# Eight attention heads scored and mixed in a row, one PSUM ring of seven banks, and weight transfers moved at a change of layers

## The reference, cut to what matters

```
for i in range(6):
    x = attn_layer(shift_tokens(x), Wqkv[i], q_scale[i], k_scale[i], Wo[i]) + x
    x = ffn_layer(shift_tokens(x), ln_g[i], ln_b[i], W1[i], b1[i], W2[i], b2[i]) + x

attn_layer: q, k, v of 16 heads of 64; q and k are normalised, scaled and rotated
            sim = 8 * q k^T over windows of 64 queries and 128 keys, masked; softmax; out = attn v; out @ Wo
ffn_layer:  layer norm; h = xn @ W1 + b1; a * gelu(gate) @ W2 + b2   (inner size 682)
```

## Time and profile before

| what | value |
|---|---|
| median of 3 runs | 2676.1 us (2675.84 to 2676.21) |
| the profiled execution, its own time | 2678.44 us |
| its span | 2676.6 us |
| PE busy | 2590.3 us, 97% |
| DVE, ACT, POOL busy | 85%, 77%, 52% |
| mean granted TensorE clock | 0.989 |
| DMA, mean | 95 GB/s |

### The profile page before, as it was taken

One profiled execution on the slowest core, in us unless ns is written; L12 is line 12 of the kernel. 1 busy time (PEld: TensorE's weight loads), 2 busy tenths in 40 slices (PEclk: granted clock), 3 DMA queues, 4 the chain that ended last, 5 costly groups with the idle time before them and its releaser, 6 DMA issues.

```text
span 2676.6 us, 77877 instructions
## 1 busy us (share of the span) xinstructions
PE 2590.3 (97%) x25160; PEld 2304.0 (86%) x25160; DVE 2279.7 (85%) x7689; ACT 2060.1 (77%) x6056; POOL 1386.8 (52%) x1438
## 2 busy tenths in 40 slices
PE   8889999999999999999999999999999999999996
PEld 7768888888888888888888888888888888888886
DVE  5579989988998888899888989988898998888883
ACT  5468878877887777788877878877888888787774
POOL 5454545545464555455464645545454645555560
PEclk9999999999999999999999999999999999999998
DMA  5212232433223333322234232244222242311110
GB/s 172 75 52 92 71 117 91 140 97 126 92 70 110 116 106 122 117 90 72 98 129 157 71 116 86 77 150 143 89 73 97 92 158 68 97 32 31 42 27 26
DMA packets 149541, 253.24 MB, mean 95 GB/s; under 512 B 21418, under 2 KB 88202, under 8 KB 148106
## 3 DMA queue, kind: packets, MB, share of 16 engines
q1 hardware_dynamic: 148698, 250.90, 28.8%
q10 hardware_dynamic: 688, 0.39, 0.1%
HBM read 137.14 MB, written 80.55 MB: 81 GB/s over the span
## 4 chain that ended last, share of the span: by engine, by line
PE 87%; DVE 2%; issue 2%; DMA 1%; POOL 1%; SPq 1%; ACT 1%; DVEq 0%; ACTq 0%; POOLq 0%
PE ring L1123 29%; PE ring L1173 14%; PE acc L1148 10%; PE score L1214 7%; PE acc L1186 6%; PE ring L1227 6%; PE ring L1137 6%; PE mix L1241 4%; PE mix L1245 2%; PE mix L1243 2%; PE ring L1157 1%; DMA xn<-res 1%; PE ring L1105 1%; PE acc L1193 0%; DVE probs L1599 0%
## 5 line engine op out<-in xcount | busy, mean ns | idle before, releaser
L1123 PE MATMUL ring<-w_qkv,xT 128*128 128x512 f32 x3456 | 888.3, 402 | 5.8 <-DVE with_sin L1506 4.5
L1123 PEld LDWEIGHTS ring<-w_qkv,xT 128*128 128x128 f32 x3456 | 627.7, 190 | 133.5 <-DVE with_sin L1506 6.1
L1408 POOL TENSOR_SCALAR sums_sq<-sums_sq 128x8 f32<-128x8 f32 x384 | 109.1, 284 | 1078.6 <-DVE sums_sq L1501 1070.3
L1344 ACT ACTIVATE probs<-probs,shift 128x128 f32<-128x128 f32 x1536 | 596.6, 392 | 25.9 <-DVE shift L1583 25.2
L1583 DVE CUSTOM_DVE_ANT_0 probs<-score,mask,query_scale 128x128 f32<-128x128 f32 x1536 | 438.5, 346 | 42.2 <-PE score L1214 34.9
L1173 PEld LDWEIGHTS ring<-nT,w_up 128*128 128x128 f32 x3168 | 395.8, 189 | 21.4 <-issue 6.8
L1173 PE MATMUL ring<-nT,w_up 128*128 128x256 f32 x3168 | 409.6, 282 | 4.2 <-issue 3.6
L1289 ACT ACTIVATE with_sin<-ring 128x512 f32<-128x512 f32 x384 | 228.2, 595 | 212.8 <-PE ring L1123 212.8
L1417 POOL TENSOR_TENSOR sums_sq<-sums_sq,half 128x8 f32<-128x8 f32 x192 | 323.2, 1683 | 16.0
L1414 POOL TENSOR_TENSOR query_scale<-sums_sq,half 128x8 f32<-128x8 f32 x192 | 318.1, 1657 | 22.0 <-POOL sums_sq L1408 11.8
L1362 ACT COPY probsT<-ring 128x512 f32<-128x512 f32 x384 | 226.4, 594 | 100.9 <-issue 95.6
(11 more groups left out here) (153 smaller groups left out, 4424.4 us busy)
## 6 DMA issues: line engine op xcount, KB each, us to landing
w_parts_scratch<-staging SPq DMA_DIRECT2D x120, 519.0 KB, 3.1
staging<-in_w_next SPq DMA_DIRECT2D x60, 519.0 KB, 5.0
w_qkv<-w_parts_scratch SPq DMA_DIRECT2D x20, 1536.0 KB, 9.1
v_mid<-v SPq DMA_DIRECT2D x192, 128.0 KB, 2.3
w_up<-w_parts_scratch SPq DMA_DIRECT2D x20, 640.0 KB, 6.1
y_in<-y_scratch SPq DMA_DIRECT2D x48, 256.0 KB, 3.0
res<-y_scratch SPq DMA_DIRECT2D x48, 256.0 KB, 2.7
y_scratch<-res SPq DMA_DIRECT2D x41, 256.0 KB, 3.2
```

What stands on the lines that cost most here:

```text
L1123: last = pe.matmul(bank(item)[:], xT[a][:, h, t * P:(t + 1) * P], w_qkv[w][:, h, c, g, :], start=(h == 0 and (a, w) == PASSES[0]), stop=(h ...
L1344: last = act.activation(probs[:, k, cols], probs[:, k, cols], ACT.Exp, bias=shift[:, k, i:i + 1], scale=-1.0, accum_out=sums[:, k, i:i + 1])
```

## The change

Three things are done.

1. **Order.** The four quads are taken in twos: `scores 0` and `scores 1` stand next to each other, then `mix 2` and `mix 3` of the sequence before; later `scores 2`, `scores 3`, `mix 0`, `mix 1`. Both `mix 2` and `mix 3` are now done a slot later. `shift`, `sums`, `probs` and `probsT` hold eight heads in place of four. The lists of ACT and DVE are rewritten to suit; POOL's stays. (`gelu_table` in ACT's list emits nothing.)
2. **Banks.** Scores (two fills each) and mixes (one each) go through the ring, which has seven banks, with 49 fills a slot. `bank_free` has the two new kinds.
3. **Transfers.** The slot after a change of layers (8L+1, `new=True`) is written out for SP alone. The fetches of blocks 3, 4 and 5 move from slot 8L+8 to it: 3 and 4 behind the load of `res`, 5 behind the three shifting copies. The first two chunk loads of the next layer move from slot 8L+1 to slot 8L+8, behind the fetch of block 2. The program also gets a smaller scratch for dynamic DMAs, which none of these transfers uses.

```diff
-RING = 4
+RING = 7
 PE_ORDER = [
-    ("scores", 0), ("mix", 3), ("unit", 1, 0), ("unit", 1, 1), ("project_out", 0), ("unit", 1, 2), ("unit", 1, 3),
-    ("project_out", 1), ("turn", 1, 0), ("turned", 0, 0), ("turned", 0, 1),
-    ("scores", 1), ("mix", 0), ("turn", 1, 1), ("unit", 1, 4), ("unit", 1, 5), ("turn", 1, 3), ("turned", 1, 0), ("turn", 1, 2),
-    ("input",), ("turned", 1, 1), ("norm_turn",),
-    ("scores", 2), ("mix", 1), ("unit", 0, 0), ("gate", 0), ("gate", 1), ("unit", 0, 1), ("gate", 2), ("value", 0),
+    ("scores", 0),
+    ("scores", 1), ("mix", 2), ("mix", 3), ("unit", 1, 0), ("unit", 1, 1), ("unit", 1, 2), ("unit", 1, 3), ("project_out", 0),
+    ("project_out", 1), ("unit", 1, 4), ("unit", 1, 5), ("input",), ("turn", 1, 2), ("turn", 1, 0), ("turn", 1, 1),
+    ("turned", 0, 0), ("turned", 0, 1), ("turned", 1, 0), ("unit", 0, 0), ("turned", 1, 1), ("turn", 1, 3), ("norm_turn",),
+    ("scores", 2),
+    ("scores", 3), ("mix", 0), ("mix", 1), ("unit", 0, 1), ("gate", 0), ("gate", 1), ("unit", 0, 2), ("gate", 2), ("value", 0),
...
 ACT_ORDER = [
-    ("out", 3), ("unit", 1, 0), ("exp", 0, 0), ("unit", 1, 1), ("exp", 0, 1), ("unit", 1, 2), ("unit", 1, 3), ("scale", 0, 1),
-    ("split_high", 0, 0), ("copied", 0, 0), ("split_high", 0, 1), ("copied", 0, 1), ("turn", 1, 0), ("exp", 1, 0),
-    ("exp", 1, 1), ("turn", 1, 1), ("unit", 1, 4), ("unit", 1, 5), ("turn", 1, 3), ("copied", 1, 0), ("turn", 1, 2), ("out", 0),
+    ("out", 2), ("exp", 0, 0), ("out", 3), ("unit", 1, 0), ("exp", 0, 1), ("unit", 1, 1), ("split_high", 0, 0), ("unit", 1, 2),
+    ("exp", 1, 0), ("exp", 1, 1), ("unit", 1, 3), ("unit", 1, 4), ("unit", 1, 5), ("input",), ("scale", 0, 1), ("copied", 0, 0),
+    ("turn", 1, 2), ("copied", 0, 1), ("turn", 1, 0), ("turn", 1, 1), ("unit", 0, 0), ("copied", 1, 0), ("copied", 1, 1),
+    ("turn", 1, 3), ("norm_turn",), ("exp", 2, 0), ("out", 0), ("exp", 2, 1), ("out", 1), ("exp", 3, 0), ("unit", 0, 1),
...
 DVE_ORDER = [
-    ("mask", 0, 0), ("mask", 0, 1), ("out", 3), ("rotate", 1, 0), ("rotate", 1, 1), ("scale", 0, 0), ("inverse", 0, 1),
-    ("rotate", 1, 2), ("add_out",), ("rotate", 1, 3), ("mask", 1, 0), ("mask", 1, 1), ("norm_stats",), ("scale", 1, 0),
+    ("mask", 0, 0), ("mask", 0, 1), ("mask", 1, 0), ("out", 2), ("mask", 1, 1), ("out", 3), ("rotate", 1, 0), ("rotate", 1, 1),
+    ("scale", 0, 0), ("inverse", 0, 1), ("rotate", 1, 2), ("add_out",), ("rotate", 1, 3), ("scale", 1, 0), ("input",),
+    ("norm_stats",), ("scale", 1, 1), ("split_low", 0, 0), ("norm_apply",), ("rotate", 0, 0), ("mask", 2, 0), ("norm_turn",),
...
+assert len(RING_FILLS) % RING == 0
+RING_BANK = [_at % RING for _at in range(len(RING_FILLS))]
...
-def run_slots(eng, slot):
+def run_slots(eng, slot, apart=False):
...
-        with eng.Fori(1 if layer else 2, BATCH - 1) as b:
+        if layer and apart:
+            slot(Slot(layer * BATCH + 1, layer, next_batch=2, ffn_batch=0, chunk=0 if layer < DEPTH - 1 else None, new=True))
+        with eng.Fori(1 if layer and not apart else 2, BATCH - 1) as b:
...
-                if s.chunk is not None:
+                if s.new:
+                    fetch(3, s.layer - 1)
+                    fetch(4, s.layer - 1)
+                if s.chunk is not None and not s.new:
                     for h in range(SLOT_CHUNKS):
                         W.load_chunk(sp, s.layer, s.chunk, h)
...
+                if s.new:
+                    fetch(5, s.layer - 1)
                 if s.late:
                     load_mid(n, 1)
...
                 if s.switch == "ffn":
                     fetch(2, s.layer)
+                    if s.layer + 1 < DEPTH - 1:
+                        for h in range(SLOT_CHUNKS):
+                            W.load_chunk(sp, s.layer + 1, 0, h)
...
-                if s.switch == "ffn":
-                    fetch(3, s.layer)
-                    fetch(4, s.layer)
...
                 if s.switch == "ffn":
-                    fetch(5, s.layer)
                     load_params(s.layer + 1)
...
-                wait(pe, scores_masked, H)
-                pe.sem_inc(passed, 1)
+                for half in range(2):
+                    bank_free(s, item, half)
+                    pe.sem_inc(passed, 1)
...
-                pe.wait_ge(probs_scaled[j], s.n * 4 + k + 1)
+                pe.wait_ge(probs_scaled[2 * (k % 2) + j], s.n * 2 + k // 2 + 1)
```

More of the change, by code:

```diff
@@ L79 @@
+    ("turned", 3, 1),
 ]
 ACT_ORDER = [
-    ("out", 3), ("unit", 1, 0), ("exp", 0, 0), ("unit", 1, 1), ("exp", 0, 1), ("unit", 1, 2), ("unit", 1, 3), ("scale", 0, 1),
-    ("split_high", 0, 0), ("copied", 0, 0), ("split_high", 0, 1), ("copied", 0, 1), ("turn", 1, 0), ("exp", 1, 0),
-    ("exp", 1, 1), ("turn", 1, 1), ("unit", 1, 4), ("unit", 1, 5), ("turn", 1, 3), ("copied", 1, 0), ("turn", 1, 2), ("out", 0),
-    ("input",), ("copied", 1, 1), ("norm_turn",), ("exp", 2, 0), ("unit", 0, 0), ("exp", 2, 1), ("gate", 0), ("unit", 0, 1),
@@ new lines @@
+    ("turn", 1, 2), ("copied", 0, 1), ("turn", 1, 0), ("turn", 1, 1), ("unit", 0, 0), ("copied", 1, 0), ("copied", 1, 1),
+    ("turn", 1, 3), ("norm_turn",), ("exp", 2, 0), ("out", 0), ("exp", 2, 1), ("out", 1), ("exp", 3, 0), ("unit", 0, 1),
+    ("split_high", 0, 1), ("gelu_table",), ("gate", 0), ("unit", 0, 2), ("gate", 1), ("gate", 2), ("unit", 0, 3), ("value", 0),
+    ("copied", 2, 0), ("exp", 3, 1), ("value", 1), ("unit", 0, 4), ("rest_high",), ("split_high", 1, 0), ("split_high", 1, 1),
@@ L88 @@
+    ("copied", 2, 1), ("scale", 3, 0), ("value", 2), ("unit", 0, 5), ("turn", 0, 2), ("turn", 0, 1), ("turn", 0, 0),
     ("turn", 0, 3), ("copied", 3, 0), ("copied", 3, 1),
@@ L115 @@
         _at[_item[2]] = len(_at) + 1
-    if _item[0] in ("unit", "turn", "turned", "input", "norm_turn", "gate", "value"):
-        for _half in range(HALVES if _item[0] == "input" else 1):
-            RING_FILLS.append((_item, _half))
-            if _item == ODD_FILL:
-                RING_BANK.append((_next + RING // 2) % RING)
-            else:
-                RING_BANK.append(_next)
-                _next = (_next + 1) % RING
-assert _next == 0
+    if _item[0] in ("unit", "turn", "turned", "input", "norm_turn", "gate", "value", "scores", "mix"):
+        RING_FILLS += [(_item, _half) for _half in range(2 if _item[0] in ("input", "scores") else 1)]
+assert len(RING_FILLS) % RING == 0
+RING_BANK = [_at % RING for _at in range(len(RING_FILLS))]
 VALUES_DONE = [max(UNIT_AT[g][4], UNIT_AT[g][5]) for g in range(GROUPS)]
@@ L138, in is_filled @@
         return -1 <= n < STEPS - 1
-    if kind == "turned":
+    if kind in ("turned", "scores") or kind == "mix" and item[1] < 2:
         return 0 <= n < STEPS
@@ L194, in does @@
         if kind in ("mix", "out"):
-            return self.attend if item[1] < 3 else not (isinstance(self.n, int) and self.n <= 0)
+            return self.attend if item[1] < 2 else not (isinstance(self.n, int) and self.n <= 0)
         if kind in ("split_high", "split_low"):
@@ L880, in layers @@
         ring = [ctx.enter_context(nc.psum_tensor(f"ring{i}", [P, GROUP], FP32)) for i in range(RING)]
-        score = [ctx.enter_context(nc.psum_tensor(f"score{i}", [P, GROUP], FP32)) for i in range(2)]
-        mix = ctx.enter_context(nc.psum_tensor("mix", [P, 2, TOKENS], FP32))
         acc = T["acc"]
@@ L1213, in quad_scores @@
                             at = k * BAND + (w // 2) * P
-                            last = pe.matmul(score[side][sides[w % 2], at:at + P], qT[rows, pair, w * WINDOW:(w + 1) * WINDOW],
+                            last = pe.matmul(bank(item, side)[sides[w % 2], at:at + P], qT[rows, pair, w * WINDOW:(w + 1) * WINDOW],
                                              kT[rows, pair, first:first + P], start=True, stop=True)
@@ L1368, in copy_out @@
                     wait(act, attn_projected, s.n)
-                act.copy(oT[0][:, pair:pair + 2, :], mix[:]).then_inc(out_high, 2)
+                act.copy(oT[0][:, pair:pair + 2, :], wide_bank(("mix", item[1]))).then_inc(out_high, 2)
             def slot(s):
```

137 lines of the change are left out of this document (72 added, 65 removed).

## The result

The changed kernel takes 2729.37 us (median of 4 runs, 2725.72 to 2731.85), the kernel before 2675.97 beside it (4 runs, 2675.09 to 2676.21): 1.0199 of before, 95% interval 1.0181 to 1.0217. It is 53 us slower where 37 us faster was forecast, and outside the range. The profiled execution took 2725.72 us, its span is 2723.6.

What follows compares the result with a forecast made beforehand. PE, busy 97% of the span, was taken as the bound. Steady slots -14 us, moved transfers -22, start and end -1 made -37: 2639 us, range 2588 to 2672 (likeliest case 2615 to 2655, chance 0.55).

Steps and rivals of the forecast that it cites:

- the 1.4: PE's forecast loss per slot in us, ahead of the second turned group and scores 2, waiting for ACT's copies.
- the floor: Steady slot without the small waits and with half the changes of shape: 49.85 us, before the new wait.
- Change of shape: PE loses 0.47 us per scores-and-mix block switching array shapes; two blocks instead of four save 0.94 us a slot.
- the rival that these changes stay: Waits and increments ahead of scores items drain the array like a shape change: 2653 to 2660 us, chance 0.10.
- Small waits: PE's waits ahead of mix 0 (0.38 us) and from input to scores 2 (0.39) go in each slot.
- The new wait: ACT's copies come late for turned 0 1 and scores 2, so PE loses 1.4 us in each slot.
- Moved transfers: Chunks loaded a slot earlier end ACT's stall at split_high 0 0 after layer changes: -22 us, bounds -26 and -5.
- Start and end: First two slots wait less for banks, the last has one mix more: -1 us, between -8 and +5.
- The slower rival: Late shifting copies delay DVE's rotate 0 0, whose bank scores 3 takes; 2685 us at 1.1 us late, chance 0.10.

Runs made afterwards that it cites:

- e1: The changed kernel with SP issuing the last layer's x2 load ahead of its wait for rest_high and the rest moves: 2671.38 us, 0.9978 of before.
- e10: e9 with one wait and one increment fewer on PE ahead of scores 0: 2655.91 us, 0.9923 of before.
- e8: e3 with ACT doing split_high 0 1 behind copied 0 1 instead of ahead of it: 2654.45 us, 0.9912 of before.
- e2: e1 with ACT's scale 0 1 moved ahead of unit 1 4, from behind input: 2669.65 us, 0.9973 of before.
- e12: e10 with out 3 ahead of rotate 1 0 on DVE again, as in the changed kernel: 2657.87 us, 0.9935 of before.
- e3: The kernel before with the moved transfers alone; lists, banks and probabilities as before: 2656.11 us, 0.9921 of before.
- e9: e2 with DVE's rotate 1 0 ahead of out 3, and turn 1 3 earlier on PE and ACT: 2662.29 us, 0.9948 of before.
- e7: e5 with turn 1 3 earlier on PE and ACT, and PE's slots written out in place of loops: 2750.58 us, 1.0274 of before.
- e5: e2 with norm_turn between scores 3 and mix 0 on PE, doubled bank waits left to the later one: 2767.23 us, 1.0334 of before.

## Why the prediction was wrong

**The step that failed** is the sentence "The rest of the new list I followed the same way for bank readers and found PE ahead of a reader by some tenths at most". It was said of one steady slot and of bank readers alone, and then multiplied by 46. Two things stand outside it.

*The last layer, +58 us.* The sum gave slots 41 to 46 the same 51.25 us as the others; they take 60.9 each. Six of the 46 slots carry a load and an addition that the other forty don't have, behind `rest_high`, which the new ACT list puts 8.6 us later in the slot (45.9 against 37.3). The wait passes over four queues: ACT, SP, POOL, PE. I followed PE, ACT and DVE, and looked at SP for the layer changes only. e1 shows the cause by itself: 2729.37 to 2671.38.

*The steady slot, +0.9 us.* Forecast 51.25, measured 52.14 as the sum of the items. By the table of items: the waits ahead of `turned 0 1` and `scores 2` 0.25 more than the 1.4 (0.50 and 1.15): the copy of `kT` ends at 25.16 us of the slot, where 25.2 was forecast, but PE starts 0.39 behind its end, which the sum had at nothing. Further, `turned 3 1` 0.29; four gates and values 0.12; two items before the slot's end 0.08; the remaining 0.15 is spread over the list (without these losses the items sum to 50.00, the floor was 49.85). The 0.29 is the second wait and increment ahead of `scores 0`: e10 takes 0.25 of it away.

The other steps, in order:

- **Change of shape: right.** 0.47 a block forecast. `scores 0` to the end of `mix 3` now takes 3.86, against 1.03 + 0.87 + 0.95 + 1.00 = 3.85 forecast. So the rival that these changes stay is refuted.
- **Small waits: right that they go, wrong that the first was PE's to win.** e8 removes the 0.38 ahead of `mix 0` in the old list and gains no more than noise. It was slack of a chain over DVE and ACT that ends at `turned 1 1`; that this chain sets the slot there is read from the trace, no run moved it. The 0.39 ahead of `scores 2` wasn't tried alone.
- **The new wait: mechanism and place right, size near, rank wrong.** Both gaps are there, ended by ACT, at the forecast times. But taking the first away (e2) gains nothing that can be told from noise, since the layer norm over POOL lets `scores 2` start only 0.28 us earlier, and `rotate 0 0` on DVE holds `scores 3`. With the copy of `kT` 1.26 us earlier (e12) the median slot is still 51.90. The Trainium skill, TensorEngine Tiling (Array Packing), PSUM Bottleneck, says that the copying out of PSUM may become the bound when TensorE gets faster. The trace agrees for ACT's two waits (0.50 and 1.15 us a slot), but what comes up behind them is first a chain of POOL that reads no PSUM.
- **Moved transfers: right.** -22 forecast, -21 measured (e3). No low clock at the changes. In ordinary slots ACT waits 2.8 us at `split_high 0 0` without an echo on PE, as said.
- **Start and end: right within its bounds.** -1 forecast; slot 0 gives 3.9 and the end takes 0.7 of it back (in e1 the end gives 1.7).
- **The slower rival** had the sign, but its mechanism isn't what made the change slower: PE waits for `rotate 0 0` some tenths in single slots, 4 times for 0.7 us in all between 1100 and 2200 us. It is real all the same. As soon as `scores 2` comes earlier the wait is there in nearly every slot (e9: 14.2 us, 45 times; e10: 13.7, 46; e12: 14.1, 46). I had given slower 0.10.

The sum, told again with what was measured: 2639 + 58 for the last layer + 0.9 by 46 = 41 makes 2738, and slot 0 with the 5 written-out slots of 51.6 us takes some of the last 9 back.

**Left open:** why written-out slots on PE cost more (e7), and whether a list exists in which the new grouping beats the old order with the moved transfers. A list with ACT, DVE and POOL all rearranged around `scores 2` wasn't tried. One piece of it stands out in the traces, the length of `ln_rstd` (last section): of the ten looped slots of layers 0 to 4 in e12 where it is short, seven take 51.2 to 51.4 us, less than the 51.57 of the old order.

## What to carry to other kernels

A slot of a hand-ordered kernel is not one slot: list the kinds (first, last layer, after a change) and follow the moved instructions in each through every queue they release, DMA queues too, before multiplying. Where the engine that seems to be the bound has small gaps, look for the chain that ends at them and what else ends within some tenths of it; taking one gap away is worth only the distance to the next chain. e2 and e8 each gained almost nothing from a wait that did vanish. Follow a gain beyond the item where it was made: in e12 `scores 2` came 0.44 us earlier and `mix 0` didn't. When all fills share a ring of banks, moving one fill changes whose reader later fills wait for (e5: 1.69 us in each slot).

## What the runs showed of the hardware

The same POOL instruction (`ln_rstd`, 128x2) takes 0.72 to 0.87 us in all 48 of its places before, but 1.41 us in 15 of 48 after, in 27 of 48 in e2 and in 20 of 48 in e12. It stands on the chain to `scores 2` and to `rotate 0 0`, and when it is long DVE stands 0.61 us for it, so slots of e12 differ by 0.6 us with it. All the long ones have DVE's `split_low` (L345 in after, a `tensor_tensor` over 128x519) running beside them. Of the 372 places in the fourteen traces without it none is long, of the 300 with it 204 are. So `split_low` beside it goes with the long time; that it is the cause isn't shown, since no run moved it alone, and what decides between long and short beside it stays open.

Two waits with two increments ahead of a group of matmuls cost 0.29 us where a loop of layers 0 to 4 starts its next pass (0.82 against 0.53), one of each 0.04 (0.57). In the slots that are written out in the change they cost nothing (0.53), nor in the loop of the last layer in e1. In e7, with all slots written out, those that had been looped take 0.62.

PE starts `scores 2` 0.39 us behind the end of ACT's copy of `kT` by the profile (median in after), but `turned 1 1` in e8, which needs no more of ACT's copy than the bank, 0.05 us behind its end (1139.61 to 1139.66).
